# Output projection of the attention heads in high and low parts, with the buffers rearranged

## The reference

```
q, k, v = the heads' projections of LN(x)            # 16 heads of 64
y = softmax(causal(q k^T) / 64) v                    # head by head
z = einsum('dvh,bhcv->bcd', W, y) / 16 * sqrt(2)     # the heads' projection
out = x + z + MoE(LN(x))                             # 32 experts of 64, top 6, and a shared one
```

## Time and profile before

| | |
|---|---|
| median of 3 runs | 1231.97 us (1231.7 to 1233.96) |
| the profiled execution | 1234.41 us, its span 1232.6 us |
| PE, PEld busy | 1203.0 us (98%), 906.4 us (74%) |
| DVE, ACT, POOL busy | 984.0 us (80%), 821.0 us (67%), 413.5 us (34%) |
| mean granted clock of TensorE | 0.996 |

### The profile page before, as it was taken

One profiled execution on the slowest core, in us unless ns is written; L12 is line 12 of the kernel. 1 busy time (PEld: TensorE's weight loads), 2 busy tenths in 40 slices (PEclk: granted clock), 3 DMA queues, 4 the chain that ended last, 5 costly groups with the idle time before them and its releaser, 6 DMA issues.

```text
span 1232.6 us, 25198 instructions
## 1 busy us (share of the span) xinstructions
PE 1203.0 (98%) x9532; PEld 906.4 (74%) x9532; DVE 984.0 (80%) x1900; ACT 821.0 (67%) x2174; POOL 413.5 (34%) x372
## 2 busy tenths in 40 slices
PE   8999999999999999999999999999999999998997
PEld 6777677767786778677867776778677767777875
DVE  5878588968896889688968896889687877788785
ACT  6775577567755775577557655765677667676775
POOL 2326410630073007200720072017201859226910
PEclk9999999999999999999999999999999999899999
DMA  7004200410041004000400140015001500000000
GB/s 253 2 29 143 83 2 29 134 48 2 29 146 36 2 29 151 31 2 30 156 25 1 34 159 18 2 39 163 10 1 40 170 1 2 10 11 18 2 10 27
DMA packets 44280, 64.01 MB, mean 52 GB/s; under 512 B 8128, under 2 KB 18368, under 8 KB 43904
## 3 DMA queue, kind: packets, MB, share of 16 engines
q1 hardware_dynamic: 44160, 62.39, 15.9%
HBM read 59.48 MB, written 2.88 MB: 51 GB/s over the span
## 4 chain that ended last, share of the span: by engine, by line
PE 83%; DVE 7%; ACT 4%; POOL 3%; issue 1%; SPq 1%; DMA 1%; POOLq 0%; DVEq 0%
PE psum L1422 15%; PE psum L1394 14%; PE psum L1444 12%; PE psum L64 10%; PE psum L66 10%; PE psum L65 10%; PE psum L1483 4%; PE psum L1399 2%; ACT probs L737 2%; PE psum L1347 1%; PE psum L1448 1%; DVE mneg L1097 1%; DVE stats L1206 1%; PE psum L1658 1%; DVE probs L1147 1%
## 5 line engine op out<-in xcount | busy, mean ns | idle before, releaser
L737 ACT ACTIVATE probs<-psum,mneg 128x512 f32<-128x512 f32 (+3 forms) x640 | 329.9, 529 | 143.9 <-DVE mneg L1097 139.5
L1097 DVE TENSOR_REDUCE mneg<-psum 128x2 f32<-128x1024 f32 (+2 forms) x320 | 254.3, 821 | 125.4 <-PE psum L1399 122.4
L1422 PE MATMUL psum<-ident,probs 128*128 128x128 f32 x1600 | 226.6, 279 | 9.0 <-ACT pt L758 3.7
L1088 DVE COPY pt<-psum 128x512 f32<-128x512 f32 x320 | 206.2, 683 | 30.2 <-PE psum L1422 28.0
L1422 PEld LDWEIGHTS psum<-ident,probs 128*128 128x128 f32 x1600 | 178.1, 141 | 42.7 <-issue 24.0
L545 POOL TENSOR_TENSOR qk_lo<-sg,qk_hi 128x512 fp32r<-128x512 f32 x64 | 91.8, 1439 | 169.1 <-ACT qk_hi L781 169.1
L509 POOL TENSOR_TENSOR rstd<-var,mhalf 128x4 f32<-128x4 f32 x7 | 7.1, 1011 | 407.2 <-DVE var L986 407.2
L1444 PE MATMUL psum<-pt,v_all 128*64 128x384 f32 (+5 forms) x1088 | 142.6, 412 | 0.0
L737 ACT ACTIVATION_READ_ACCUMULATOR probs<-psum,mneg 128x1 f32 x640 | 132.2, 207 | 0.0
L1394 PE MATMUL psum<-qk_hi 64*128 64x512 f32 (+7 forms) x640 | 123.0, 381 | 1.2 <-ACT probs L737 1.1
L1444 PEld LDWEIGHTS psum<-pt,v_all 128*64 128x64 f32 (+1 forms) x1088 | 69.8, 135 | 62.9 <-issue 50.6
(11 more groups left out here) (263 smaller groups left out, 2470.7 us busy)
## 6 DMA issues: line engine op xcount, KB each, us to landing
crow<-weights SPq DMA_DIRECT2D x256, 128.0 KB, 2.9
rrow<-sums SPq DMA_DIRECT2D x128, 128.0 KB, 2.9
gu_raw<-in_gu SPq DMA_DIRECT2D x1, 2176.0 KB, 11.5
x_all<-in_x SPq DMA_DIRECT2D x8, 256.0 KB, 6.2
out_rows<-x_all SPq DMA_DIRECT2D x8, 256.0 KB, 2.3
down_raw<-in_down SPq DMA_DIRECT2D x1, 1088.0 KB, 13.7
wqkv_raw<-in_wqkv SPq DMA_DIRECT2D x1, 896.0 KB, 6.8
wqkv_raw<-in_wqkv SPq DMA_DIRECT2D x1, 512.0 KB, 5.1
```

What stands on the lines that cost most here:

```text
L737: last = act.activation(probs[:, h * HALF + PROB[t]:h * HALF + PROB[t] + w], bank[score_bank(rnd, c) + h][:, o:o + w], ACT.Exp, bias=mneg[ ...
L1088: dve.tensor_copy(turned_rows(rnd)[:, s % 2, :, 3 - s // 2, :], bank[TURN_BANK[s]].rearrange("p (j q) -> p j q", q=P)).then_inc(pt_ready, 1)
L1097: last = dve.tensor_reduce(mneg_h[:, :, t], psum[:, b:b + 2, o:o + P * (t + 1)], AX, ALU.max, negate=True)
L1422: last = nc.tensor.transpose(bank[TURN_BANK[s]][:, i * P:(i + 1) * P], probs[:, v:v + P], ident[:, :])
```

## The change

The heads' projection is made like the other large products, of high and low fp32r parts: `w_out_hi` and `w_out_lo` are made once in the first batch (ACT copies, POOL subtracts), and for each batch ACT copies each divided pair into `y_hi` (`Y_HIGH_AFTER` names the units behind which it does) and POOL (pairs 0 to 3) or DVE (pairs 4 to 7) subtracts to get `y_lo`, in place over `yt`. `y_hi` lies over `pt` in reverse order. `RROWS` is 2 instead of 3, with another `SUMS_AFTER`. The copy of `ACC` moves into `sg`, and some small tiles share room or lose their second layer's copy. The second layer's mask uses the first layer's two tiles of 64 rows. In all rounds but the first of a batch (or of a group) the masks of chunks 1 and 2 now stand behind the products of both.

```diff
-RROWS = 3
+RROWS = 2
...
-        acc_cols = rrow[:, 2, :]
+        acc_cols = sg_two[:, 1, :]
...
-        SUMS_AFTER = [2, 3, 4, 8, 9, 10, 12, 13]
+        SUMS_AFTER = [2, 3, 7, 9, 10, 11, 12, 13]
...
+        Y_HIGH_AFTER = {8: [0], 11: [1, 2], 12: [3], 13: [4], 15: [5], 16: [6]}
+        POOL_Y_LO = {3: 0, 5: 1, 6: 2, 7: 3}
+        VECTOR_Y_LO = range(len(POOL_Y_LO), PAIRS)
...
+            def low_values(b, p):
+                pool.wait_ge(y_hi_ready, b * PAIRS + p + 1)
+                pool.tensor_tensor(y_lo[:, p, :], yt[:, p, :], y_hi[:, PAIRS - 1 - p, :].bitcast(F32), ALU.subtract).then_inc(pool_y_lo_ready, 1)
...
                     for p in POOL_LO[u]:
                         divide_pair(b, p)
+                        if p in POOL_Y_LO:
+                            low_values(b, POOL_Y_LO[p])
...
+            def high_values(b, p):
+                act.wait_ge(y_divided, b * PAIRS + p + 1)
+                act.activation(y_hi[:, PAIRS - 1 - p, :], yt[:, p, :], ACT.Copy).then_inc(y_hi_ready, 1)
...
                         act.activation(w_out0[:, :, :], w_out0[:, :, :], ACT.Copy, scale=OUT0).then_inc(act_setup, 1)
+                        act.wait_ge(act_setup, 1)
+                        act.activation(w_out_hi[:, :, :], w_out0[:, :, :], ACT.Copy).then_inc(w_out_hi_ready, 1)
...
+                    for p in Y_HIGH_AFTER.get(u, []):
+                        high_values(b, p)
+                high_values(b, PAIRS - 1)
                 high_part(b * UNITS + UNITS - 1, UNITS - 1)
...
                 low_part(b * UNITS + UNITS - 1, UNITS - 1)
+                if b < B - 1:
+                    low_values(b, VECTOR_Y_LO)
...
             for g in range(G - 1):
                 stats1(0, 0, g)
+                if g < 2:
+                    low_values(B - 1, VECTOR_Y_LO[2 * g:2 * g + 2])
...
+            def score_rest(rnd, buf, head_rows):
+
+                score_products(rnd, 1, buf, head_rows)
+                pe.wait_ge(exp_done, exp_count(rnd, 0))
+                score_products(rnd, 2, buf, head_rows)
+                score_masks(rnd, 2)
+                score_masks(rnd, 1)
...
             def project_out(b, i):
-                pe.wait_ge(y_divided, b * PAIRS + 2 * i + 2)
+                n = len(POOL_Y_LO)
+                if 2 * i < n:
+                    pe.wait_ge(pool_y_lo_ready, b * n + 2 * i + 2)
+                else:
+                    pe.wait_ge(y_lo_ready, b * (PAIRS - n) + 2 * i - n + 2)
                 for p in (2 * i, 2 * i + 1):
-                    last = mm(ACC, w_out0[:, p, :], yt[:, p, :], start=False, stop=(p == PAIRS - 1), **K)
+                    last = split_matmul(nc, ACC, (w_out_hi[:, p, :], w_out_lo[:, p, :]), (y_hi[:, PAIRS - 1 - p, :], y_lo[:, p, :]), False, p == PAIRS - 1, **K)
                 return last
```

More of the change, by code:

```diff
@@ L105, in build @@
         down_hi = sb("down_hi", [P, UNITS, D], F32R)
-        w_out0 = sb("w_out0", [P, PAIRS, D])
+        with ExitStack() as raw:
+            w_out0 = raw.enter_context(nc.sbuf_tensor("w_out0", [P, PAIRS, D], F32))
+        w_out_lo = sb("w_out_lo", [P, PAIRS, D], F32R)
+        w_out_hi = sb("w_out_hi", [P, PAIRS, D], F32R)
         rw_hi = sb("rw_hi", [P, E], F32R)
@@ L153, in build @@
         rrow = sb("rrow", [P, RROWS, T])
+        with ExitStack() as units:
+            y_hi = units.enter_context(nc.sbuf_tensor("y_hi", [P, PAIRS, T], F32R))
         pt = sb("pt", [P, 2, TILES, TILES, P])
+        with ExitStack() as units:
+            y_lo = units.enter_context(nc.sbuf_tensor("y_lo", [P, PAIRS, T], F32R))
         yt = sb("yt", [P, PAIRS, T])
@@ L179, in build @@
         nmr = sb("nmr", [P, TT])
-        ss1 = sb("ss1", [P, G, TILES * (H1 + KV1)])
-        rn1 = sb("rn1", [P, G, TILES * (H1 + KV1)])
+        ss1, rn1 = (v[:, :, :].rearrange("p t e -> p (t e)")[:, 0:G * TILES * (H1 + KV1)].rearrange("p (g n) -> p g n", g=G) for v in (corr, left))
         with ExitStack() as first:
@@ L313, in build @@
         y_divided = sem("y_divided")
+        w_out_hi_ready = sem("w_out_hi_ready")
+        w_out_lo_ready = sem("w_out_lo_ready")
+        y_hi_ready = sem("y_hi_ready")
+        y_lo_ready = sem("y_lo_ready")
+        pool_y_lo_ready = sem("pool_y_lo_ready")
         y_done = sem("y_done")
@@ L551, in units, with split_w_out @@
                         divide_pair(b, p)
+                        if p in POOL_Y_LO:
+                            low_values(b, POOL_Y_LO[p])
+            def split_w_out():
+                pool.wait_ge(w_out_hi_ready, 1)
+                pool.tensor_tensor(w_out_lo[:, :, :], w_out0[:, :, :], w_out_hi[:, :, :].bitcast(F32), ALU.subtract).then_inc(w_out_lo_ready, 1)
             def split_down(k):
@@ L601, in _ @@
                 split_gu(k)
-            second_layer_masks()
+            second_layer_ones()
+            split_w_out()
             for k in range(len(DOWN_PIECES)):
@@ L977, in stats0 @@
                 for t in range(TILES):
-                    last = dve.bn_stats(stats[:, b * TILES + t, :], x_all[:, b, t, :])
+                    last = dve.bn_stats(stats[:, t, :], x_all[:, b, t, :])
                 chain.step(last)
@@ L983, in variances0 @@
                 for t in range(TILES):
-                    last = dve.bn_aggr(mv[:, b * TILES + t, :], stats[:, b * TILES + t, :])
+                    last = dve.bn_aggr(mv[:, b * TILES + t, :], stats[:, t, :])
                 chain.step(last)
@@ L1147, in hidden, with low_values @@
                 dve.tensor_tensor(sg[u % 3], sg[u % 3], crow[:, m % CROWS, :], ALU.mult).then_inc(hm_ready, 1)
+            def low_values(b, pairs):
+                for p in pairs:
+                    dve.wait_ge(y_hi_ready, b * PAIRS + p + 1)
+                    dve.tensor_tensor(y_lo[:, p, :], yt[:, p, :], y_hi[:, PAIRS - 1 - p, :].bitcast(F32), ALU.subtract).then_inc(y_lo_ready, 1)
             def add_rows(b):
@@ L1205, in row_stats @@
                 for t in range(TILES):
-                    last = dve.bn_stats(stats[:, b * TILES + t, :], src[:, t, :])
+                    last = dve.bn_stats(stats[:, t, :], src[:, t, :])
                 chain.step(last)
                 for t in range(TILES):
-                    last = dve.bn_aggr(mv[:, b * TILES + t, :], stats[:, b * TILES + t, :])
+                    last = dve.bn_aggr(mv[:, b * TILES + t, :], stats[:, t, :])
                 chain.step(last)
@@ L1383, in project_values, with score_products @@
                     split_matmul(nc, bank[4 + f % 2], (xt_hi[:, b % 2, c], xt_lo[:, b % 2, c]), w, True, True).then_inc(v_done, 1)
-            def score_chunk(rnd, c, buf, head_rows, later, hide):
+            ROWS0 = [slice(0, DQ), slice(DQ, 2 * DQ)]
+            def score_products(rnd, c, buf, head_rows):
                 hi, lo = qk_hi[:, buf, :, :], qk_lo[:, buf, :, :]
-                k = head_rows[0].stop - head_rows[0].start
                 for i, t in enumerate(CHUNKS[c]):
@@ L1394, in score_chunk, with score_masks @@
                             mm(bank[score_bank(rnd, c) + h][:, o:o + w], ql[r, 0, qs_], kl[r, 1, ks], start=i == 0 and n == 0, stop=False, **K)
+            def score_masks(rnd, c):
                 for t in CHUNKS[c]:
                     o = SCORE_COL[t] + P * t
-                    for piece in range(P // k):
-                        for h, r in enumerate(head_rows):
-                            last = mm(bank[score_bank(rnd, c) + h][:, o + piece * k:o + (piece + 1) * k], later[r, piece, :], hide[r, :],
+                    for piece in range(P // DQ):
+                        for h, r in enumerate(ROWS0):
+                            last = mm(bank[score_bank(rnd, c) + h][:, o + piece * DQ:o + (piece + 1) * DQ], later0[r, piece, :], hide0[r, :],
                                       start=False, stop=True, **K)
                 last.then_inc(scored, 1)
+            def score_chunk(rnd, c, buf, head_rows):
+                score_products(rnd, c, buf, head_rows)
+                score_masks(rnd, c)
+            def score_rest(rnd, buf, head_rows):
[4 more added lines that the diff above has]
+                score_masks(rnd, 1)
             def turn_step(rnd, s):
@@ L1643, in _ @@
                 if b == 1:
-                    pe.wait_ge(act_setup, 1)
+                    pe.wait_ge(w_out_lo_ready, 1)
                 for p in range(PAIRS):
@@ L1783, in output_rows, with head_rows1 @@
                     last.then_inc(rows_done, 1)
+                def head_rows1(r):
+                    return [slice((2 * (r % 2) + h) * HD1, (2 * (r % 2) + h + 1) * HD1) for h in range(2)]
                 def score1(r, c):
-                    head_rows = [slice((2 * (r % 2) + h) * HD1, (2 * (r % 2) + h + 1) * HD1) for h in range(2)]
-                    score_chunk(ROUNDS0 + n0 * 2 + r, c, (n0 + r // 2) % 2, head_rows, later1, hide1)
+                    score_chunk(ROUNDS0 + n0 * 2 + r, c, (n0 + r // 2) % 2, head_rows1(r))
                 pe.wait_ge(qk_lo_ready, (ROUNDS0 + n0) * 2 + 2)
```

22 lines of the change are left out of this document (6 added, 16 removed).

## The result

The changed kernel takes 1242.72 us (median of 5 runs, 1241.29 to 1243.55), the kernel before 1233.32 us in the same comparison: the ratio is 1.0072, 95% interval 1.0055 to 1.0089. It is slower, by little but clear of the noise. The prediction was 1239 in a range of 1225 to 1246.

The account below looks back on a forecast made before the run. PE was taken to bound the first layer. Terms -8.7, -4.3, -1.4, +1.1, +13.8, +0.5, +6.5 sum to +7.5 us: 1234.4 to 1241.9 profiled, less 2.4 for the median, about 1239; range 1225 to 1246.

Parts of the forecast that it names:

- What bounds: First layer, 130 to 1000 us: PE is busy 868.51 of 870 us, so its waits lengthen the kernel us for us.
- The projection: Heads of batches 1 to 7: three fp32r products replace four passes, 0.155 us gained a pair, 56 pairs, -8.7 us.
- The masks: Score slots: one change from masks to products fewer, 0.09 us in 48 slots, -4.3 us; second layer -1.4.
- the masks save nothing: Rival: the cost sits in the products, or 64-row masks over 32-row products cost more; 1244 to 1246 us, chance 0.07.
- Making the parts: First batch: ACT makes w_out_hi, +1.1 us; ACT's copies into y_hi and DVE's low parts count at nothing.
- POOL's chain: Batch heads: nine POOL operations after pair 4's load take 14.4 us; PE waits 2.3 in six batches, +13.8; batch 1 +0.5.
- What is late next: Batch heads: unit 16's high part is ready about 628.0 us, PE wants it about 629.8, so it is hidden.
- The last batch: PE waits 3.8 us more for unit 11's low part, DVE's low parts add up to 2.8 in the statistics: +6.5.
- The sum: Whole kernel: all terms give +7.5 us, 1234.4 to 1241.9 of the profiled execution, about 1239 against the median.
- Faster: Rival: POOL is in time at batch heads, 1.25 to 1.35 us an operation; 1223 to 1226, up to 1229; chance 0.27.
- balance: Rival: POOL's operations average about 1.45 us, a 0.9 us wait in each of six batches; about 1231 us, chance 0.17.
- Much slower: Rival: POOL stands still for each whole 0.69 us DVE operation, a 4.0 us wait in six batches; 1251 us, chance 0.07.

Follow-up runs that it names:

- masks_old: The changed kernel with the masks of chunks 1 and 2 each behind its own products again: 1249.95 us, ratio to before 1.0141.
- project_late: The changed kernel with project_out(1) moved on PE from behind unit 14 to behind chunk 0: 1242.67 us, ratio to before 1.0079.
- dve_low_11: As dve_low, and with pair 4 divided behind unit 11's low part: 1229.87 us, ratio to before 0.9975.
- no_pool_low: The changed kernel without POOL's low parts of pairs 0 to 3, part of the computation left out: 1225.69 us, ratio to before 0.9938.
- dve_low: The changed kernel with low parts of pairs 2, 3 on DVE, project_out(1) behind chunk 0, ACT's unit 16 high part before pair 7's: 1231.92 us.
- loads_alone: The kernel before with two of three buffers of inverse sums and the changed list of load places, nothing else: 1233.83 us, ratio 1.0005.

## Why the prediction was right

**What bounds** held: each us that PE waited at a batch's head was a us of the batch (and 0.27 more), and the kernel without POOL's low parts gave them all back.

**The projection**, -8.7 by the sum: 1.31 us a head, 7 heads, -9.2. Of each 1.31, 0.03 are the masks' (heads without a wait are 18.81 us in masks_old).

**The masks**, -4.3: this term was mis-sized. The slots gained 0.04 us, and the one in the head 0.03; for six in each of 8 batches that is -1.9, and on the kernel before it was even less. The product of 64x256 behind masks took 0.21; I set it against 0.115, the step of the products that follow it. In the changed trace the same product stands behind other products and takes 0.17 (173.08 to 173.25 in the timeline of this slot):

```profile
173.08 0.34 PE L1438 MATMUL psum<-qk_hi 64*128 64x256 f32 x2
173.25 0.28 PE L1438 MATMUL psum<-qk_lo,qk_hi 64*128 64x256 f32 x2
```

So 0.055 of the 0.09 is the product's own. It was the rival "the masks save nothing" in part. The second layer's -1.4 measured -0.5 in one group, -1.0 if the other gained as much.

**Making the parts**, +1.1: batch 1 begins at 135.6 to 136.1 in the three traces with before's projection and at 136.4 to 138.1 in the ten with the new one, 1.6 us apart in the mean, so about the size. In the pair of traces compared here it is only 0.3 (136.12 and 136.44). ACT's copies cost nothing that shows.

**POOL's chain**, +13.8: right in its mechanism and place, in batch 5 landing 10.05 us ahead of s against 10.0, chain 14.0 against 14.4, batch 1 free of a wait. The six waits cost 9.8 + 6 x 0.27 = 11.4 us, not 13.8, for two reasons of like size. The load landed 9.84 to 10.66 us ahead of s, 10.33 in the mean (10.66 in batch 4, wait 1.17; 9.84 in batch 2, wait 2.40); a single batch was a poor sample for six. And the chain took 14.2 in the mean; in batch 5 three of its operations, not two, went undisturbed. With the clock's 1.5 behind the longest it is 12.9. That the wait could cost clock stood in the prediction for the last batch only.

**What is late next** was right that unit 16 is hidden, but only as long as PE waits for POOL. I had its parts ready at 628.0, 4.7 us behind s; DVE ended them at 630.5, 5.1 behind s. I had counted the price of the meeting on POOL alone and let DVE keep its 0.69. project_late shows the waits of up to 1.8 us that stand behind; no term or rival had them.

**The last batch**, +6.5: PE waits 3.44, 3.1 more than before (3.8 by the sum), and its units are 3.3 us longer. Behind them come 2.2 more, which contain the masks' estimated -1.0, so about 6.5 in all. The units' half comes with the loads alone (39.94 us); the other half came with the rest of the change, and no run separates it.

**The sum**, +7.5, against 8.5 between the two spans. That it came so close is partly luck: a gain of the masks that was 2.8 us too large and waits that were 2.4 too large nearly cancelled, and the clock's 1.5 behind a wait and the 1.0 of batch 1's slot stood in no term. The forecast of 1239 is 3.7 below the result, half of it because it took off 2.4 for the profiled execution, which after the change stands only 0.5 above the median.

**The rivals.** "Faster" and "balance" asked for 1.35 or 1.45 us an operation; the nine took 14.0 / 9 = 1.56. "Much slower" asked that a DVE operation add all of its 0.69 to POOL's; it adds 0.46 (1.29 to 1.75). The Trainium skill's page SBUF - State Buffer, section Who interferes with whom, has the two engines shut each other out for whole instructions. The trace agrees for DVE: L1175 grows by 1.1 us (0.68 to 1.79) beside POOL operations that take 1.29 alone, and L1067 of 0.29 by 1.5. For POOL it leaves the question open. POOL pays 0.46, two thirds of a DVE operation of 0.69, but its operation of 620.84 begins 0.60 us before L1175 ends (619.65 + 1.79 = 621.44), so that it may wait for the rest of an instruction already under way. The rival fell by the size of POOL's share, which the sum had rightly from the row of 3.45.

## What to carry to other kernels

When work goes to a helper engine, count its chain from the last outside event it waits for to the product that needs it, with the durations it has beside a busy neighbour, and count what the neighbour loses by the meeting too. Taking one operation out of such a chain gains nothing if another load or result starts the rest of it; look for the event from which the engine is never idle again. And here the order of a list was worth as much as the arithmetic: with the same projection the kernel lost 9 us or gained 5.5, by the places of eight loads and a few operations: two subtractions, one division, one copy of ACT's and one of the four projections.

## What was unexpected of the hardware

The half-speed stretches cost about 1.7 us or a multiple of it: without the last one, the profiles here sum to 0, 1.7, 3.4, 5.2, 6.8 and 11.9 us. At a batch's head all waits of 2.21 to 2.48 us were followed by one (five waits, in three kernels), and none of 0.8 to 1.8 us. In the last batch it is less simple: waits of 3.44 and 3.46 us were followed by one in project_late and masks_old, one of 1.89 us was in dve_low_11, but those of 3.08 to 3.45 in the changed kernel, in no_pool_low and in dve_low, and of 2.28 in loads_alone, were not. In the second layer a wait of 1.39 us was followed by one in the kernel before, and one of 1.27 in dve_low_11 but not in dve_low. So the length of the wait isn't all of it, and what else decides was not tried. The spread of masks_old's times (12.8 us) is of the size of such stretches, but only one of its executions was profiled.
